# A prologue rearranged: sums of convolution weights in their own memory, ScalarE normalising, block routing first, a second recurrence unit ahead of the tiles

## The reference

```python
xn = layernorm(x)
x = x + rwkv(xn) + moe(xn)            # layer 0
xn = layernorm(x)
x = x + block_conv(xn) + ternary(xn)  # layer 1
```

## Time and profile before

| | us |
|---|---|
| median of 3 runs (408.34 to 410.1) | 410.06 |
| the profiled execution: its own time | 404.66 |
| its span | 402.7 |
| mean granted clock of PE, share of full | 0.979 |
| busy: PE / DVE / POOL / ACT | 356.4 / 281.7 / 230.3 / 133.8 |

### The profile page before, as it was taken

One profiled execution on the slowest core, in us unless ns is written; L12 is line 12 of the kernel. 1 busy time (PEld: TensorE's weight loads), 2 busy tenths in 40 slices (PEclk: granted clock), 3 DMA queues, 4 the chain that ended last, 5 costly groups with the idle time before them and its releaser, 6 DMA issues.

```text
span 402.7 us, 6493 instructions
## 1 busy us (share of the span) xinstructions
PE 356.4 (88%) x1444; PEld 246.5 (61%) x1445; DVE 281.7 (70%) x425; ACT 133.8 (33%) x274; POOL 230.3 (57%) x182
## 2 busy tenths in 40 slices
PE   0569997999999998899989899979979929999996
PEld 0528786555665554554456546645558818888886
DVE  3982858299999999999999989422290888426124
ACT  1344336262431523315225252122220588000023
POOL 2120477975838888989889818867888730000000
PEclk9989999999999999999999999999999968999999
DMA  6792124388695565676755895697562320000005
GB/s 213 265 349 88 52 104 130 125 311 264 184 387 152 177 200 153 184 191 168 179 172 167 233 378 160 183 365 263 185 189 73 100 59 0 2 0 2 0 28 182
DMA packets 43494, 66.62 MB, mean 165 GB/s; under 512 B 4688, under 2 KB 23760, under 8 KB 43472
## 3 DMA queue, kind: packets, MB, share of 16 engines
q1 hardware_dynamic: 32448, 54.27, 43.1%
q10 hardware_dynamic: 9488, 7.88, 6.2%
q0 software_dynamic: 1536, 4.20, 3.2%
HBM read 56.76 MB, written 9.57 MB: 165 GB/s over the span
## 4 chain that ended last, share of the span: by engine, by line
POOL 44%; PE 21%; DMA 15%; DVE 6%; issue 5%; ACT 3%; POOLq 3%; SPq 2%; DVEq 0%; ACTq 0%
POOL acc L469 38%; DMA ring<-blocks 12%; PE pg L856 4%; POOL slots_x L454 4%; PE pt L856 3%; PE pu L856 3%; DVE acc L911 2%; PE pr L856 2%; PE py L856 2%; DMA acc<-x 2%; POOL acc L459 2%; POOLq L469 1%; PE pg L838 1%; PE pu L838 1%; ACT big L650 1%
## 5 line engine op out<-in xcount | busy, mean ns | idle before, releaser
L469 POOL TENSOR_TENSOR acc<-acc,ring 128x512 f32 x128 | 183.5, 1434 | 47.6 <-DMA ring<-blocks 25.7
L745 PE MATMUL pg<-big,xs_t 128*128 x144 | 68.7, 599 | 2.5 <-issue 2.5
L768 PE MATMUL py<-big,h_t 128*128 x288 | 65.9, 382 | 5.2 <-ACT h_t L553 5.1
L768 PEld LDWEIGHTS py<-big,h_t 128*128 128x128 f32 x288 | 54.1, 190 | 22.5 <-issue 16.0
L745 PE MATMUL pu<-big,xs_t 128*128 x144 | 67.7, 592 | 0.0
L1062 DVE SCALAR_TENSOR_TENSOR th<-th,pu 128x512 f32<-128x512 f32 x36 | 24.3, 675 | 35.0 <-ACT th L558 34.8
L745 PEld LDWEIGHTS pu<-big,xs_t 128*128 128x128 f32 x144 | 27.4, 190 | 34.4 <-issue 34.4
L558 ACT ACTIVATE th<-pg 128x512 f32<-128x512 f32 x36 | 21.6, 599 | 62.1 <-PE pu L745 62.1
L745 PEld LDWEIGHTS pg<-big,xs_t 128*128 128x128 f32 x144 | 24.6, 190 | 21.5 <-issue 21.2
L454 POOL DMA_INDIRECT slots_x<-acc,pos_i x16 | 16.5, 1032 | 25.9 <-DVE eid_i L961 21.3
L754 PEld LDWEIGHTS pt<-ident,h 128*128 128x128 f32 x144 | 17.0, 141 | 20.7 <-DVE h L1065 15.0
(11 more groups left out here) (279 smaller groups left out, 596.5 us busy)
## 6 DMA issues: line engine op xcount, KB each, us to landing
ring<-blocks SPq DMA_DIRECT2D x128, 256.0 KB, 2.9
big<-w_g SPq DMA_DIRECT2D x4, 1024.0 KB, 6.5
big<-w_u SPq DMA_DIRECT2D x4, 1024.0 KB, 9.0
big<-w_d SPq DMA_DIRECT2D x4, 1024.0 KB, 11.6
slots_x<-h SPq DMA_DIRECT2D x1, 2688.0 KB, 9.8
xs<-slots_x ACTq DMA_DIRECT2D x19, 128.0 KB, 3.3
slots_y<-y_sb ACTq DMA_DIRECT2D x18, 128.0 KB, 3.2
acc<-x SPq DMA_DIRECT2D x4, 512.0 KB, 7.4
```

The costliest lines, as they stand in the source:

```text
L469: g.tensor_tensor(a, a, ring[:, place, :].rearrange("p (j o) -> p j o", j=TAPS), ALU.add)\
L745: mm = t.matmul(dst[:, :], xs_t[:, par, k, :], big[:, ds(e * per_e + (w_at + k * FF + 512 * f), 512)], start=(k == 0), stop=(k == KC - 1))
L768: mm = t.matmul(py[:, 0:C], h_t[:, k, :], big[:, ds(e * per_e + (down_at + k * C), C)], start=(k == 0), stop=(k == KF - 1))
```

## The change

Names and places only; every operation still runs once.

- x, `xn` and W_rvk lie in the memory of experts 0 and 1 (`big`) and not in `acc`. POOL clears `acc` in one memset right behind its two small subtractions, ahead of the scatter, and starts its adds as soon as the scatter is issued.
- SP: W_rvk is loaded between the first and the second part of x; the zeros no longer wait for small loads; the ring's first four blocks, and then expert 0, are loaded in the prologue. Experts 1, 2 and 3 are loaded in three parts each with a round of four refills between parts.
- `xn` is made by ACT (Identity with scale and bias) and not by DVE; the x_hi copies stand between.
- DVE does the block routing first, and its last seven operations stand between the one-hot choice and `pos_i`. PE does three or four pieces ahead of the logits; six PSUM banks take pieces and not seven.
- Unit 1 of the recurrence stands ahead of the tiles on DVE. Its `exps` and `scaled` on ACT stand behind piece 23. PE now does 23 pieces ahead of the wait for the first slot tile (22 before).

```diff
-        acc = sb("acc", [P, acc_cols + KC * 3 * C])
-        x_in = acc[:, 0:NT * C].rearrange("p (i c) -> p i c", i=NT)
-        xn = acc[:, NT * C:2 * NT * C].rearrange("p (i c) -> p i c", i=NT)
+        acc = sb("acc", [P, acc_cols + MW])
+        x_in = big[:, 0:NT * C].rearrange("p (i c) -> p i c", i=NT)
+        xn = big[:, per_e:per_e + NT * C].rearrange("p (i c) -> p i c", i=NT)
...
-        EXPS_AT = 12
-        SLOTS_AT = 22
+        EXPS_AT = (15, RP * ROUNDS)
+        SLOTS_AT = 23
+        SOFTMAX_AT = 8
...
# SP
-            load_expert(0)
+            for n in range(RING):
+                sp.dma_start(ring[:, n, :], blocks[n]).then_inc(s_bk[n], 16)
+            sp.wait_ge(s_xn, NT)
+            for q in range(3):
+                load_part(0, q)
             sp.wait_ge(s_sc, 16 * NT)
             sp.dma_start(xs[:, :], slots_x[0:P, :]).then_inc(s_xs, 16)
...
             expert_here(0)
             refills(1, 2)
-            sp.wait_ge(s_xs, 32)
-            load_expert(1)
-            refills(2, 5)
-            expert_here(1)
             sp.wait_ge(s_rv, RP * ROUNDS)
-            load_expert(2)
-            refills(5, 8)
+            turn = 2
+            for e in (1, 2):
+                for q in range(3):
+                    load_part(e, q)
+                    refills(turn, turn + 1)
+                    turn += 1
+                if e == 2:
+                    expert_here(1)
+            refills(turn, turn + 2)
             expert_here(2)
...
# POOL
+            g.wait_ge(s_wh, 1)
+            g.tensor_tensor(w_lo, wrvk_sb[:, :, :], w_hi.bitcast(F32), ALU.subtract).then_inc(s_wl, 1)
             g.wait_ge(s_wh, 2)
             g.tensor_tensor(wr_2[:, :, NE:], wr_sb[:, :, :], wr_2[:, :, 0:NE].bitcast(F32), ALU.subtract)\
                 .then_inc(s_wl, 1)
-            g.tensor_tensor(w_lo, wrvk_sb[:, :, :], w_hi.bitcast(F32), ALU.subtract).then_inc(s_wl, 1)
+            g.memset(acc[:, :], 0.0).then_inc(s_ba, 1)
...
-            g.wait_ge(s_sc, 16 * NT)
-            g.wait_ge(s_tp, NT // 2)
-            step(g, g.memset(acc[:, 0:acc_cols], 0.0))
             g.wait_ge(s_cv, 1)
-            g.wait_ge(s_rv, RP * ROUNDS)
-            g.memset(acc[:, acc_cols:acc_cols + MW], 0.0).then_inc(s_ba, 1)
...
# ACT
+                if m == 1:
+                    a.wait_ge(s_wr, 16)
+                    a.activation(w_hi, wrvk_sb[:, :, :], ACT.Copy).then_inc(s_wh, 1)
+                a.wait_ge(s_rs, m + 1)
+                for i in range(4 * m, 4 * m + 4):
+                    a.activation(xn[:, i, :], x_in[:, i, :], ACT.Identity, bias=nmr[:, i:i + 1],
+                                 scale=rstd[:, i:i + 1]).then_inc(s_xn, 1)
+                if m:
+                    high(2 * m - 2)
+                    high(2 * m - 1)
+            a.wait_ge(s_c, 16 * N_SMALL)
+            a.activation(wr_2[:, :, 0:NE], wr_sb[:, :, :], ACT.Copy).then_inc(s_wh, 1)
+            high(6)
+            high(7)
...
-            for q in range(RP * ROUNDS):
+            for q in range(RP * ROUNDS + 1):
...
+                if q == EXPS_AT[1]:
+                    exps(1, 1)
+                    scaled(1, 1)
+                if q < RP * ROUNDS:
+                    piece(q // RP, q % RP, six[q % 6])
             def all_tiles(unit):
-                tile(0, 0, unit((1, 1)), first_tile=True)
+                tile(0, 0, first_tile=True)
...
# PE
+            for n in range(4):
+                turn_pair(n)
+            t.wait_ge(s_wh, 1)
             t.wait_ge(s_wl, 1)
+            pieces(0, 2)
+            turn_pair(4)
+            turn_pair(5)
+            pieces(2, 3)
+            turn_pair(6)
+            turn_pair(7)
+            pieces(3, 4)
+
+            t.wait_ge(s_wl, 2)
...  (the logits, four groups)
+            pieces(4, 5)
+            t.wait_ge(s_lc, 3)
+            t.wait_ge(s_fb, 1)
+            t.matmul(py[:, 0:P], first_b, before[:, :], start=True, stop=True).then_inc(s_gp, 1)
+            pieces(5, 6)
+            t.wait_ge(s_lc, ROUNDS)
...  (the folds, 16 tiles)
             mm.then_inc(s_lg, 1)
-            pieces(2, 4)
+            pieces(6, 7)
+            t.wait_ge(s_gd, 1)
...  (four matmuls of the block routing)
+            pieces(7, 8)
             t.wait_ge(s_oh, 1)
...
-            pieces(12, SLOTS_AT)
+            pieces(8, SLOTS_AT)
...
# DVE: block routing moved up, in two runs of instructions
+            moments(0)
+            scales(0)
+            moments(1)
+            scales(1)
+            moments(2)
+            scales(2)
+            low(0)
+            low(1)
+            moments(3)
+            scales(3)
+            for n in range(2, NT // 2):
+                low(n)
...
             v.wait_ge(s_c, 16 * N_SMALL)
+            step(v, v.tensor_scalar(slot_i[:, :], rows_i[:, :], 1, None, ALU.arith_shift_right))
...  (L963 to L982, then wait_ge(s_gp, 1), then L988 to L993)
             v.wait_ge(s_lg, 1)
...  (L924 to L936)
+            v.wait_ge(s_gt, 1)
...  (L995 to L1002)
             v.wait_ge(s_cn, 1)
...
-            wkv(0, 0, 0, (0, UNIT), j_static=True)
+            for c in range(KC):
+                wkv(c, 0, c, (0, UNIT), j_static=True)
             def all_tiles(unit):
                 for s in range(LOOP):
-                    tile(s, unit((1, 0, 1)), *PARTS[s], j_static=True)
+                    tile(s)
```

More of the change, by code:

```diff
@@ L211, in build @@
         four = [pg[0], pu[0], pg[1], pu[1]]
-        seven = pt + [py] + four
-        eight = four + pt + [py, pr]
+        six = four + pt
+        eight = six + [py, pr]
         s_x = [sem(f"s_x{n}") for n in range(4)]
         s_c = sem("s_c")
+        s_wr = sem("s_wr")
         s_zf = sem("s_zf")
@@ L498, in _, with high @@
             a.dma_start(rc_i[:, 1:2], cols.unsqueeze(1)).then_inc(s_c, 16)
[L499 to L503, removed]
-            a.activation(w_hi, wrvk_sb[:, :, :], ACT.Copy).then_inc(s_wh, 1)
-            for n in range(NT // 2):
+            def high(n):
                 a.wait_ge(s_tp, n + 1)
@@ L618, in _ @@
             with a.If(e9 > NE - 2):
-                exps(1, 1)
-                scaled(1, 1)
                 with a.Fori(1, ROUNDS) as j:
@@ L679, in _, with turn_pair @@
             t.wait_ge(s_k, N_CONST)
-            for n in range(NT // 2):
+            def turn_pair(n):
                 t.wait_ge(s_xn, 2 * n + 2)
@@ L712, in _ @@
                                   start=(n == 0), stop=(n == 2 * KC - 1))
                 mm.then_inc(s_lt, 1)
-            t.wait_ge(s_wl, 2)
-            pieces(0, 2)
-            for g in range(ROUNDS):
-                t.wait_ge(s_lc, g + 1)
-                for i in range(4 * g, 4 * g + 4):
-                    mm = t.matmul(pr[:, NE * i:NE * i + NE], lg_t[:, i * P:(i + 1) * P], fold[0:2 * NE, :],
-                                  start=True, stop=True)
-            mm.then_inc(s_lg, 1)
@@ L723, in _ @@
-            pieces(2, 4)
+            pieces(4, 5)
[4 more added lines that the diff above has]
+            t.wait_ge(s_lc, ROUNDS)
+            for i in range(NT):
+                mm = t.matmul(pr[:, NE * i:NE * i + NE], lg_t[:, i * P:(i + 1) * P], fold[0:2 * NE, :],
+                              start=True, stop=True)
+            mm.then_inc(s_lg, 1)
@@ new lines, in _ @@
+            step(v, v.tensor_copy(rowf, rp_i[:, :]))
+            step(v, v.tensor_copy(colf, rc_i[:, 1:2]))
+            step(v, v.tensor_scalar(same, key, keyc, None, ALU.is_equal))
+            step(v, v.scalar_tensor_tensor(out=odd, in0=slot_i[:, :], scalar=-2.0, in1=rows_i[:, :],
+                                           op0=ALU.mult, op1=ALU.add))
+            step(v, v.tensor_copy(rows_i[:, :], slot_i[:, :]))
+            step(v, v.tensor_tensor(tmp, same, after, ALU.mult))
+            step(v, v.tensor_reduce(seenc, tmp, AX.X, ALU.add))
@@ new lines, in _ @@
+            step(v, v.tensor_scalar(firstc, seenc, 0.0, None, ALU.is_equal))
+            v.tensor_scalar(first_b, ones[:, :], firstc, None, ALU.mult).then_inc(s_fb, 1)
+            step(v, v.tensor_tensor(tmp, same, iota_r, ALU.mult))
+            step(v, v.tensor_reduce(fidx, tmp, AX.X, ALU.max))
+            step(v, v.tensor_scalar(fidx, fidx, -1.0, float(P), ALU.mult, ALU.add))
+            step(v, v.tensor_scalar(same, iota, fidx, None, ALU.is_equal))
+            v.wait_ge(s_gp, 1)
+            step(v, v.tensor_tensor(tmp, same, py[:, 0:P], ALU.mult))
@@ L923, in _ @@
+            step(v, v.tensor_reduce(gid, tmp, AX.X, ALU.add))
+            step(v, v.tensor_scalar(gid_d, ident[:, :], gid, None, ALU.mult))
+            step(v, v.tensor_scalar(row_b, ones[:, :], rowf, None, ALU.mult))
+            step(v, v.tensor_scalar(col_b, ones[:, :], colf, None, ALU.mult))
+            v.tensor_scalar(sel, iota[:, 0:MACROS], gid, firstc, ALU.is_equal, ALU.mult).then_inc(s_gd, 1)
             v.wait_ge(s_lg, 1)
@@ L937, in _ @@
             ins.then_inc(s_oh, 1)
+            v.wait_ge(s_gt, 1)
```

(8 more changed lines are left out.)

171 lines of the change are left out of this document (72 added, 99 removed).

## The result

| us | before | after |
|---|---|---|
| median, 4 runs each | 409.2 (406.68 to 410.1) | 422.55 (421.75 to 427.22) |
| the profiled execution: its own time, span | 404.66, 402.7 | 422.35, 420.7 |
| mean granted clock of PE | 0.979 | 0.959 |

Ratio 1.036, 95% interval 1.027 to 1.045: the change makes the kernel slower, by 18.0 us between the spans of the two profiled executions and 13.4 between the medians. The ratios, unlike the medians, leave out executions that are more than 1.5% above the fastest of their kernel, most of them at a slightly lower clock (2 of 4 in experiment 2, 3 of 6 in 4, 5 of 10 in 5, 4 of 12 in 9, 1 of 12 in 10, 4 of 6 in 11), and as the profiles of experiments 4, 5, 9 and 11 are of such executions, I compare stretches inside them, not their ends.

The account below looks back on a forecast made before the run. DVE was taken to pace the tile loop, with DVE and POOL holding each other up. Terms 1.8 + 4.9 + 1.3 + 6.8 + 3 - 2.6 = +15.2 us gave a median of 425.3, range 409 to 431.

Parts of the forecast that it names:

- The case of the block with unit 1 late: Main case: POOL's memset blocks DVE's block routing and unit 1 delays tile 0; 425.3 us, chance 0.46.
- the first scatter at 50 to 53: Sign for the main case: the first scatter comes at 50 to 53 us.
- The memset against the block routing: Prologue: DVE's tensor_scalar waits until POOL's memset ends, +4.9 us, and PE's wait behind it adds +1.3.
- PE sits at the first routing matmul meanwhile: Prologue: PE waits while DVE is blocked, then runs a piece at the low clock, +1.3 us.
- Norm and logits: Prologue, up to the router's sum: X, the landing of the first slot tile, moves by +1.8 us.
- The clock: PE in the prologue: low clock for a piece after its wait at the first routing matmul, +1.3 us.
- Unit 1 ahead of the tiles: DVE behind X: step 3 waits for ACT's `exps`, the unit delays tile 0 and unit 2; +6.8 us, bounds +3.4, +9.7.
- Adds and loads: Tile loop: units 2 and 7 now meet POOL's adds, less some 3 us waiting for expert 3's load; +3 us.
- The end: Tail: the gathers start with the last store, as POOL finishes its adds well ahead of it; -2.6 us.
- B (no blocking): Rival, prologue: the memset does not stop DVE's small operations; +9.0 us, 419.1, chance 0.32.
- C (faster): Rival: unit 1 ends by X+8.8, when tile 0 is ready, and PE runs dense; -5.8 us, 404.3, chance 0.14.
- D: Rival, no change: low bounds everywhere, POOL's earlier start giving back the rest; 0 to +2 us, 411, chance 0.08.

Follow-up runs that it names:

- experiment 2: Changed kernel with unit 1, its `exps` and `scaled` back in tiles 0 and 1, memset whole; 419.03 us, no ratio.
- 4: Changed kernel with experts 1 and 2 loaded whole again, each followed by three rounds of refills; 425.22 us, ratio 1.030.
- 5: Changed kernel with the memset cut in nine and unit 1 back in tiles 0 and 1; 411.6 us, ratio 1.006.
- 9: Changed kernel: nine memsets, unit 1 in tiles 0 and 1, small matmul behind folds, fold matrix earlier, last seven block operations behind `eid`; 413.04 us, ratio 1.007.
- experiment 10: As experiment 9, with the other six block operations behind the router's one-hots and PE's block matmuls behind the one-hot matmuls; 411.11 us, ratio 1.008.
- 11: As experiment 9, with piece 6 (six matmuls) between the halves of the folds; 417.69 us, ratio 1.012.
- experiment 1: Changed kernel with POOL's one memset of `acc` cut in nine; 417.93 us, ratio 1.020.
- 6: Changed kernel with PE's small first routing matmul behind the folds and the fold matrix made earlier, memset whole; 416.55 us, ratio 1.024.
- experiment 7: Changed kernel with PE making all pair transposes and the logits ahead of all pieces; 422.26 us, ratio 1.038.
- 3: Changed kernel with unit 1's `exps` and `scaled` two pieces earlier on ACT, ahead of its wait for the first slot tile; 423.55 us, ratio 1.033.
- experiment 12: As experiment 10, with POOL pausing after add 104 of 128 until DVE has finished unit 7; 409.14 us, ratio 1.006.
- experiment 8: Changed kernel: nine memsets, small matmul behind folds, last seven block operations behind `eid`, `exps` ahead of pieces 12 and 20, unit 1 in front; 412.69 us, ratio 1.013.

## Why the prediction was right, and where it was off

The case of the block with unit 1 late was the right one. The sign and the range hold, and the median is close (425.3 against 422.55), but that closeness is in part luck. On the profiled executions the sum was +15.2 and the result +18.0, and this 18.0 is made of terms that missed by +3.2 (up to X), +2.9 (unit 1) and -3.0 (behind unit 7), which partly cancel. Of the signs that were named, "the first scatter at 50 to 53" did not come (55.49), nor did units of 26.7 up to the end (units 6 and 7 took 24.1 and 24.5); the others came, some of them 2 to 5 us later than said.

*The memset against the block routing, +4.9 and +1.3.* The stall is there at 4.98, to 0.1 us. Its price, 6.2 in the sum, is 3.6 to 4.4 in X (experiments 1 and 6, one profile each) and 4.6 to 6.0 in the medians. The step that failed is "PE sits at the first routing matmul meanwhile": the wait lasted 3.44, not 4.9, as pieces filled the rest, and only because the folds stood behind it did it count.

*Norm and logits, +1.8.* This term failed most. With the block and the wait away, X is still 6.7 to 7.6 later (experiments 1, 5, 6). I had the folds behind two pieces, starting near 33.5; PE's list has six ahead of them, of which I took four to fit into waits. With those four ahead the logits end at 33.4, without them at 30.7 (experiment 7): 2.7 us of them are on the path. The first two also took longer than the 1.4 us that I priced, 2.6 us each (19.85 to 25.0), the length of the piece at the low clock in the earlier trace rows, though the clock column reads 1.00 there. The router's sum was 2.7 us late even in experiment 10. The rest is in the chain from this sum to the scatter: 7.6 us before, 10.2 after, 8.5 in experiment 10, where no block operation stands in between. What part of it is the clock is open.

*The clock.* I priced it at 1.3 from one pause. The low level appeared near 40 us in every changed kernel, also where PE had hardly a wait, and in some profiles lasted till 57; X in kernels with the same prologue on PE was 80.02 (changed kernel) and 83.49, 84.98 and 85.51 (experiments 2, 4 and 3). The low level goes with it: it ended by 50 us in the first and near 56 in the others, and the folds took 4.05 us in the first and 6.98 to 6.99 in the others. That spread of 5.5 is larger than the term. What sets how long the level lasts was not found.

*Unit 1 ahead of the tiles, +6.8.* Mechanism confirmed at each step, with X+5.4 for step 3 and unit 2 at X+33.1 once the unit was back. The size was the term's upper bound, +9.7: I took 13.85 us for the rest of the unit from the earlier trace rows, but it took 16.4. DVE's and POOL's timelines show where, before and after:
```profile
90.95 0.74 DVE L1038 SCALAR_TENSOR_TENSOR big<-big,cab 128x512 f32<-128x512 f32 x1
91.81 0.75 DVE L1039 SCALAR_TENSOR_TENSOR big<-big,cab 128x512 f32<-128x512 f32 x1
92.60 0.17 DVE L1040 COPY carry<-big 128x5 f32<-128x5 f32 x1
94.19 1.27 POOL L469 TENSOR_TENSOR acc<-acc,ring 128x512 f32 x1 [5.54 <-DMA ring<-blocks]
...
90.61 1.63 DVE L1094 SCALAR_TENSOR_TENSOR big<-big,cab 128x512 f32<-128x512 f32 x1
92.34 1.56 DVE L1095 SCALAR_TENSOR_TENSOR big<-big,cab 128x512 f32<-128x512 f32 x1
93.94 1.11 DVE L1096 COPY carry<-big 128x5 f32<-128x5 f32 x1
```
Before, these three steps fell into POOL's wait of 5.54 us for the ring and took 1.66 us together; after, adds ran beside them and they took 4.30. The other steps met adds both times (the last one 1.57 and 1.55). The first tile's h so came 2.5 us later than foreseen. The low clock behind PE's wait is there (0.50 from 95 to 103 us) and was in the sum at 1.5.

*Adds and loads, +3.* +2.8 measured, but here too the number is better than its working: the parts named there, 2.7 and 4.7 less 3, make 4.4 and not 3. Measured are +2.5 in unit 2 (26.5, before 24.0), -2.5 in unit 6 (24.1, before 26.6), beside a wait of POOL for the ring of 6.45 us such as the working had foreseen, and some +2.6 in unit 7 (24.5, foreseen 26.7). And the step missed what follows. When unit 7 is slower, the stretch behind it is shorter: from its end to the issue of the last store it took 46.0 before and 43.6 after, -2.4, which the sum had at 0. In experiment 12 it is the other way round: units shorter by 7.9 us, a tail longer by 3.5. That PE's own backlog is what evens this out is likely, but was not tested alone.

*The end, -2.6.* Right in kind, and -3.1 in size: the gathers follow the store now, 0.9 us behind its landing, and the landing took 1.7 us in place of 3.0.

*The rivals.* B (no blocking) falls by the row of 4.98. C (faster) falls by `exps` behind X, as argued against it; with `exps` at 20 and 12 (experiment 8), unit 1 ended at X+13.9, still not by X+8.8. D had +2 at most.

That the adds slow DVE is plain in one line too: the last step of unit 7 takes 1.53 us with adds beside it and 0.69 in experiment 12, where POOL pauses. The Trainium skill (SBUF — State Buffer, Who interferes with whom) says that a DVE instruction with two SBUF inputs contends with a GpSimd instruction that reads; the rows agree.

## What to carry to other kernels

A long instruction of POOL on idle time is not free if DVE has a tensor_scalar in its reach (4.98 us here): cut it in pieces, or put what waits for DVE behind what PE can do at once; here either was enough. When work is moved ahead of a landmark, ask what it waits for: here a unit put "in the prologue" waited for an ACT step that was issued only behind the landmark, and then stood in front of the first tile. And count an in-order engine's list item by item between two events; pieces that "fill waits" do so only if the waits are there.

## What was not expected of the hardware

The granted clock fell near 40 us in the profile of every changed kernel, also while PE was busy 5.00 of 5.00 us (experiment 1: 0.64 and 0.68 in the stretches from 40 to 50 us, so part of each at 1.2 GHz). It stayed low for some 7 us in some and up to 20 in others, and for differing lengths in kernels with the same prologue. In the kernel before, PE was busy for only 1.73 us between 20 and 25, the clock was low there (0.73 from 25 to 30), and it stayed full from 30 to 65 us, through the same folds. Neither PE's wait (experiments 1, 6) nor the unbroken row of folds (11) explains it, and its cause is open.
